# Four-layer graph network on one core: the third layer's projections as three products of rounded halves, a shared arena, and new instruction sequences

## The reference

```python
x = _layernorm(x + _L0_gnn_ref(x, adj, ...))   # attention, 4 heads of 64
x = _layernorm(x + _L1_gnn_ref(x, adj, ...))   # tanh-scored graph layer, 4 heads of 256, gated
x = _layernorm(x + _L2_gnn_ref(x, adj, ...))   # the 32-wide layer: 8 heads of 32
x = _layernorm(x + _L3_gnn_ref(x, adj, ...))   # attention, 4 heads of 64
```

```python
m = embs @ map_w.T + map_b
n = sem / norm                                  # sem: m in heads of 32
cos = jnp.einsum('bhsd,bhtd->bhst', n, n)
cos_adj = (cos > THRESHOLD).astype(embs.dtype)  # THRESHOLD = 0.1
q = (m @ q_w.T + q_b).reshape(b, s, h, dk).transpose(0, 2, 1, 3)
k = (m @ k_w.T + k_b).reshape(b, s, h, dk).transpose(0, 2, 1, 3)
p_attn = jax.nn.softmax(scores, axis=-1) * keep
adj = cos_adj * p_attn
sem_h = (embs @ gcn_map_w.T + gcn_map_b).reshape(b, s, h, hk).transpose(2, 0, 1, 3)
out = jax.nn.relu((adj_h @ sem_h) @ gcn_W.T / (adj_h.sum(-1, keepdims=True) + 1.0))
```

## Time and profile before

| | |
|---|---|
| median of 3 runs | 2848.74 us |
| the profiled execution's own time | 2851.96 us |
| its span, first to last instruction | 2850.2 us |
| TensorE matmul busy | 94% of the span, 21265 instructions |
| VectorE, ScalarE, GpSimd busy | 70%, 48%, 33% |
| mean granted TensorE clock | 0.983 |

### The profile page before, as it was taken

The page is one execution under the profiler, slowest core; times in us unless marked ns, Lnnn a source line. Parts: engine busy times, 40 slices in busy tenths (PEclk is TensorE's granted clock), DMA queues, the critical chain, the costliest instruction groups (busy, mean ns, idle before and its releaser), DMA issues. The chain is left out here.

```text
span 2850.2 us, 61579 instructions
## 1 busy us (share of the span) xinstructions
PE 2669.7 (94%) x21265; PEld 2335.4 (82%) x21265; DVE 1991.9 (70%) x6621; ACT 1381.5 (48%) x3841; POOL 939.0 (33%) x971
## 2 busy tenths in 40 slices
PE   4789999999999999999999999999999999999985
PEld 3778888888888888888888888888888888888873
DVE  3347767777776777777677777767777776777764
ACT  0234545545454554555455445545544554554442
...
DMA packets 44480, 29.76 MB, mean 10 GB/s; under 512 B 21264, under 2 KB 44048, under 8 KB 44432
## 3 DMA queue, kind: packets, MB, share of 16 engines
...
...
## 5 line engine op out<-in xcount | busy, mean ns | idle before, releaser
L176 POOL TENSOR_SCALAR l_ve<-l_mv 128x2 f32<-128x2 f32 x128 | 42.6, 333 | 1048.7 <-DVE l_mv L161 1048.6
L1229 ACT ACTIVATE b<-b,s_sh 128x256 f32<-128x256 f32 x512 | 255.6, 505 | 109.7 <-DVE s_sh L418 109.7
L245 PE MATMUL bank<-a32r 128*128 128x256 f32 x1024 | 304.4, 297 | 3.6 <-issue 2.2
L1480 POOL TENSOR_TENSOR a32r<-a,a32r 128x512 fp32r<-128x512 f32 x128 | 180.9, 1413 | 339.8 <-ACT a32r L1179 337.4
L247 PE MATMUL bank<-a32r 128*128 128x256 f32 x1024 | 289.6, 283 | 0.0
L246 PE MATMUL bank<-a32r 128*128 128x256 f32 x1024 | 289.2, 282 | 0.0
L1485 POOL TENSOR_TENSOR a32r<-a,a32r 128x512 fp32r<-128x512 f32 x128 | 166.4, 1300 | 301.7 <-ACT a32r L1175 301.7
L418 DVE CUSTOM_DVE_ANT_0 b<-bank,s_add 128x256 f32<-128x256 f32 x512 | 185.9, 420 | 84.5 <-issue 59.2
L413 DVE TENSOR_TENSOR a32r<-bank,a32r 128x512 fp32r<-128x512 f32 x128 | 85.6, 689 | 208.2 <-ACT a32r L1216 114.9
L245 PEld LDWEIGHTS bank<-a32r 128*128 128x128 f32 x1024 | 195.2, 191 | 37.3 <-issue 22.9
L1388 DVE SCALAR_TENSOR_TENSOR b<-bank,b 128x256 f32<-128x256 f32 x512 | 188.2, 420 | 33.5 <-PE bank L1083 31.3
(11 more groups left out here) (248 smaller groups left out, 8777.2 us busy)
## 6 DMA issues: line engine op xcount, KB each, us to landing
...
```

Of the source, the lines that this page charges most:

```text
L176: pool.tensor_scalar(N.ve[:, :], N.mv[:, :, 1], LN_EPS, None, ALU.add).then_inc(N.eps.sem, 1)
L245: pe.matmul(out, w[0], x[0], start=first, stop=False)
L1229: last = act.activation(S.e[:, n, it, :], S.e[:, n, it, :], ACT.Exp, bias=S.sh[:, it, h:h + 1], scale=-1.0, accum_out=S.sums[:, it, h:h + 1])
L1480: pool.tensor_tensor(G.wh[h % 2][1], G.whf[:, h % 2, :, :], G.wh[h % 2][0].bitcast(F32), ALU.subtract).then_inc(G.wh_sb.sem, 1)
```

## The change

1. S.xt, S.w_m, S.w_q, S.w_k and S.w_s become pairs of fp32r halves. TensorE's four projections of layer S then go through the three-product branch of pe_product. ScalarE writes S.xt's hi half, and a new VectorE stage b_x_t writes its lo half (dve_lower); b_m, b_q, b_k and b_sem wait for that one. The weights' halves are made in dve_setup.
2. Layer A's probabilities, exponentials, q, k and v move from the tile a32 into the tile "arena", whose places are also seen as fp32r under the name arena_r, and there lie over buffers of layer G. a32 shrinks from 10 to 5 places, and a32r (22 places) becomes arena_r.
3. All four lists of ORDER are replaced. ScalarE's g_wh for heads 2 and 3 gets one more wait, on the product that last read the buffer it writes.

```diff
+ARENA, ARENA_AT = 22, 16512
...
     "PE": [
-        ("g_gate_x", 1), ("a_x_t", 0), ("g_ha_t", 1), ("d_k", 2), ("g_gate", 1), ("d_scores_0", 2), ("d_v", 2),
...
+        ("g_ha_3_1", 1), ("g_ha_3_0", 1), ("d_k", 2), ("g_ha_t", 1), ("a_x_t", 0), ("g_gate_x", 1), ("d_q", 2),
...
+        arena = sb("arena", [P, ARENA * T * NODES])
+        arena_r = nc.alloc_sbuf_tensor_at("arena_r", [P, ARENA * T * NODES], F32R, offset=ARENA_AT)
...
-        a32, a32r = places("a32", 10, F32), places("a32r", 22, F32R)
-        b32 = places("b32", 13, F32)
+        a32, a32r, plain = places("a32", 5, F32), places_of(arena_r), places_of(arena)
+        b32, b32r = places("b32", 13, F32), places("b32r", 2, F32R)
...
-        A.e, A.pt, A.qt, A.kt, A.v, A.xb = a32(0, 4), a32(4, 4), a32(4), a32(5), a32(8), x1
+        A.e, A.pt, A.qt, A.kt, A.v, A.xb = plain(10, 4), plain(16, 4), plain(14), plain(15), plain(8), x1
...
-        S.m, S.sq, S.u, S.xt, S.sem = (b32(n) for n in (4, 5, 6, 7, 0))
+        S.m, S.sq, S.u, S.sem = (b32(n) for n in (4, 5, 6, 0))
+        S.xt = split(b32r, 0)
...
-        S.w_m, S.w_q, S.w_k, S.w_s = (sb(f"s_w_{n}", [P, T, DIM])[:, :, :] for n in "mqks")
+        S.w_m, S.w_q, S.w_k, S.w_s = (split_sb(f"s_w_{n}", [P, T, DIM]) for n in "mqks")
...
             def g_wh(g, h):
                 act.wait_ge(G.wh_f.sem, G.wh_f.at(g, h + 1))
+                if h >= 2:
+                    act.wait_ge(G.p_psum.sem, G.p_psum.at(g, h - 1))
                 act.activation(G.wh[h % 2][0], G.whf[:, h % 2, :, :], ACT.Copy).then_inc(G.wh_hi.sem, 1)
...
-                    act.activation(S.xt, view(BB[2]), ACT.Copy).then_inc(S.x_t_sb.sem, 1)
+                    act.activation(S.xt[0], view(BB[2]), ACT.Copy).then_inc(S.x_t_hi.sem, 1)
...
+                elif stage == "b_x_t":
+                    dve.wait_ge(S.x_t_hi.sem, S.x_t_hi.at(g))
+                    dve_lower(dve, BB[2], S.xt).then_inc(S.x_t_sb.sem, 1)
```

More of the change, by code:

```diff
@@ L45 @@
 BANK = 512
+ARENA, ARENA_AT = 22, 16512
 ORDER = {
     "PE": [
-        ("g_gate_x", 1), ("a_x_t", 0), ("g_ha_t", 1), ("d_k", 2), ("g_gate", 1), ("d_scores_0", 2), ("d_v", 2),
[3 rows of a table removed]
-        ("d_out", 2), ("a_out", 0), ("b_m", 1), ("g_adj_t", 0), ("b_k", 1), ("b_sem", 1), ("g_x_t", 0), ("b_q", 1),
[7 rows of a table removed]
+        ("g_ha_3_1", 1), ("g_ha_3_0", 1), ("d_k", 2), ("g_ha_t", 1), ("a_x_t", 0), ("g_gate_x", 1), ("d_q", 2),
+        ("g_gate", 1), ("d_scores_0", 2), ("d_v", 2), ("a_k", 0), ("d_scores_1", 2), ("a_q", 0), ("a_v", 0),
+        ("a_scores_0", 0), ("d_probs_0", 2), ("d_probs_1", 2), ("d_probs_2", 2), ("d_probs_3", 2), ("a_scores_1", 0),
+        ("d_values_0", 2), ("b_x_t", 1), ("a_probs_0", 0), ("a_probs_1", 0), ("d_values_1", 2), ("a_probs_2", 0),
+        ("a_probs_3", 0), ("a_values_0", 0), ("a_values_1", 0), ("d_out", 2), ("a_out", 0), ("b_m", 1), ("b_sem", 1),
+        ("g_adj_t", 0), ("b_q", 1), ("g_x_t", 0), ("b_k", 1), ("g_z_0", 0), ("b_unit_t", 1), ("g_c", 0),
[6 rows of a table added]
+        ("d_x_t", 1),
@@ L63 @@
     ],
     "ACT": [
[L65 to L69, removed]
[4 rows of a table removed]
+        ("b_copy_6", 2), ("g_wh_3", 1), ("g_p_2", 1), ("g_s_3", 1), ("b_relu_1", 2), ("g_a_3", 1), ("g_p_3", 1),
@@ L74 @@
+        ("d_x_t", 2), ("g_ha", 1), ("d_k", 2), ("g_ha_t", 1), ("a_x_t", 0), ("d_q", 2), ("g_gate", 1),
+        ("d_exps_0", 2), ("a_k", 0), ("d_exps_1", 2), ("d_exps_2", 2), ("a_q", 0), ("d_exps_3", 2), ("d_probs_0", 2),
+        ("d_probs_2", 2), ("a_exps_0", 0), ("a_exps_1", 0), ("a_exps_2", 0), ("a_exps_3", 0), ("a_probs_0", 0),
+        ("b_x_t", 1), ("a_probs_2", 0), ("a_o_copy", 0), ("g_x_t", 0), ("b_k", 1), ("b_q", 1), ("g_z_0", 0),
[4 rows of a table added]
     ],
     "DVE": [
-        ("b_stats", 2), ("g_p_3", 1), ("b_norm_out", 2), ("g_diff", 1), ("g_ha_t", 1), ("a_x_t", 0), ("g_gate", 1),
@@ L77 @@
-        ("d_mask_0", 2), ("g_mix", 1), ("g_sum", 1), ("d_mask_1", 2), ("d_v", 2), ("g_stats", 1), ("d_norm_p_0", 2),
[3 rows of a table removed]
-        ("d_stats", 2), ("a_sum", 0), ("b_m", 1), ("a_stats", 0), ("b_square", 1), ("a_norm_out", 0), ("g_x_t", 0),
-        ("b_unit", 1), ("b_sem", 1), ("g_z_0", 0), ("g_adj_t", 0), ("b_mask_0", 1), ("g_c", 0), ("b_mask_1", 1),
[5 rows of a table removed]
-        ("b_factors", 1), ("g_p_2", 0), ("b_scale", 1), ("b_sum", 1),
+        ("b_factors", 2), ("b_copy_5", 2), ("b_copy_7", 2), ("g_p_2", 1), ("g_a_3", 1), ("b_scale", 2), ("b_sum", 2),
@@ L89 @@
+        ("b_stats", 2), ("b_norm_out", 2), ("g_p_3", 1), ("g_diff", 1), ("a_x_t", 0), ("g_ha_t", 1), ("g_gate", 1),
+        ("d_mask_0", 2), ("g_mix", 1), ("d_v", 2), ("g_sum", 1), ("d_mask_1", 2), ("g_stats", 1), ("d_mask_2", 2),
[3 rows of a table added]
+        ("d_sum", 2), ("a_sum", 0), ("a_stats", 0), ("b_m", 1), ("b_square", 1), ("a_norm_out", 0), ("d_stats", 2),
+        ("g_x_t", 0), ("b_sem", 1), ("b_unit", 1), ("g_z_0", 0), ("g_c", 0), ("b_mask_0", 1), ("b_mask_1", 1),
[5 rows of a table added]
     ],
     "POOL": [
-        ("g_wh_3", 2), ("g_a_3", 2), ("b_rstd", 3), ("b_mask", 2), ("g_x_ha", 2), ("g_adj", 1), ("g_rstd", 2),
@@ L92 @@
-        ("d_bias", 3), ("b_keep", 2), ("a_bias", 1), ("d_mask", 2), ("a_rstd", 1), ("b_inorm", 2), ("d_rstd", 3),
-        ("g_wh_0", 1), ("g_a_0", 1), ("g_a_1", 1), ("a_mask", 0), ("g_wh_1", 1), ("g_a_2", 1), ("g_wh_2", 1),
-        ("b_sums", 2),
+        ("g_wh_2", 2), ("g_a_2", 2), ("b_sums", 3), ("g_wh_3", 2), ("g_a_3", 2), ("b_mask", 2), ("b_rstd", 3),
+        ("b_keep", 2), ("g_x_ha", 2), ("a_mask", 1), ("a_bias", 1), ("d_bias", 3), ("g_adj", 1), ("g_rstd", 2),
+        ("a_rstd", 1), ("b_inorm", 2), ("g_wh_0", 1), ("g_a_0", 1), ("g_wh_1", 1), ("d_rstd", 3), ("d_mask", 2),
@@ L95 @@
+        ("g_a_1", 1),
     ],
@@ L529, in build @@
         C.ident, C.ident_bf = sb("ident", [P, P]), sb("ident_bf", [P, P], BF16)
-        C.ones, C.minus_one, C.minus_half = sb("ones", [P, P]), sb("minus_one", [P, 16]), sb("minus_half", [P, 16])
+        C.minus_one, C.minus_half = sb("minus_one", [P, 16]), sb("minus_half", [P, 16])
         x_in, x_loaded = sb("x_in", [P, T, DIM]), signal("x_loaded", 16)
@@ L544, in places, with places_of @@
         def places(name, count, dt):
-            t = sb(name, [P, count * PLACE], dt)
+            return places_of(sb(name, [P, count * PLACE], dt))
+        def places_of(t):
             def at(first, n=1):
@@ L644, in build @@
         W = Names()
[L646 removed]
+        C.ones = plain(20)[:, 0, 0:P]
+        W.w, W.attn, W.r = a32(0, 4), plain(10, 4), b32(0, 4)
         W.a_w = b32(0, 4).rearrange("p h t n -> p (h t n)").rearrange("p (t n) -> p t n", t=T)
[L648 removed]
+        W.fc, W.g1, W.g2, W.map, W.q, W.k, W.gm = plain(8), plain(9), b32(4), b32(5), b32(6), b32(7), b32(8)
         W.g1_t, W.q_t, W.k_t = W.g1, W.q, W.k
@@ L760, in c_bias @@
                 for kc in range(T):
-                    last = pe.matmul(b[:, 0:HG], C.ones[:, :], W.ab[:, kc, :], start=(kc == 0), stop=(kc == T - 1))
+                    last = pe.matmul(b[:, 0:HG], C.ones, W.ab[:, kc, :], start=(kc == 0), stop=(kc == T - 1))
                 return last
@@ L791, in dve_setup @@
             for jt in range(T):
-                dve.tensor_scalar(W.gb_rows[:, jt, :], C.ones[:, :], W.gb[:, jt:jt + 1], None, ALU.mult)
+                dve.tensor_scalar(W.gb_rows[:, jt, :], C.ones, W.gb[:, jt:jt + 1], None, ALU.mult)
             for h in range(HG):
@@ L1468, in _ @@
             pool.memset(C.minus_half[:, :], -0.5).then_inc(const_ready, 1)
-            pool.memset(C.ones[:, :], 1.0).then_inc(const_ready, 1)
+            pool.memset(C.ones, 1.0).then_inc(const_ready, 1)
             pool.wait_ge(const_ready, 3)
```

5 lines of the change are left out of this document (2 added, 3 removed), and 40 rows, old and new, of the table ORDER.

## The result

The changed kernel takes **2815.09 us**, the median of 4 runs (2814.03 to 2816.07), against 2848.89 for the kernel before on the same chip (2847.84 to 2849.53): a ratio of 0.9882, 95% interval 0.9865 to 0.9899, 34 us less. The forecast was 2804 and faster, with a range of 2755 to 2838. So the sign and the range held and the size was 11 us too good. The attribution behind it was worse than the sum, as the experiments show.

What follows compares the result with a forecast made beforehand. TensorE's sequence with short waits was taken as the bound: -1.32 projections, -0.3 waits, +0.2 edges, -1.42 us a period, -44 over 31; +1 setup, -2 fill and drain gave 2807, less 3.2 to the median 2804 us, range 2755 to 2838.

Steps and rivals of the forecast that it cites:

- What bounds the kernel: Whole body: one long TensorE sequence with short waits, 3.5 us of waits in a period of 83.36 us.
- The term of the projections: Layer S's four projections on TensorE: 1.40 us each instead of 1.73, gaining 1.32 us a period (0.88 to 1.44).
- eaten at g_x_t: Rival: shorter projections cover less of the chain from a_out, g_x_t waits 1.0 us longer; 2835 us, chance 0.17.
- The waits: TensorE's waits under the new lists: 3.2 us a period in sum against 3.5 before, a gain of 0.3.
- d_probs_2: TensorE's wait for VectorE's a_v, g_norm_out (1.05) and d_norm_p_1 (0.86): 0.7 to 0.8 us, before 0.95.
- a_probs_0: TensorE's new wait for VectorE's a_mask_2, a_mask_3 and 0.86 of a_norm_p_0 (2.15 us): 0.6 us.
- b_values_1: TensorE's new wait because b_factors (1.35 us) now precedes VectorE's b_copy_5 and b_copy_7: 0.55 us.
- slower, by GpSimd: Rival: GpSimd's new run of stages ends 2 us later, g_p_1 waits 1.8 us a period; 2861 us, chance 0.05.
- The other work: TensorE: scores of D and A no longer neighbours, one more block of small products, about +0.2 us a period.
- Setup, fill and drain: Outside the full periods: +1 us for setup copies (0 to 2.8), -2 us for fill and drain.
- The last step: From profiled execution to median: 3.2 us taken off 2807, giving 2804 us.
- tests named beforehand: Signs: period 81.9 us, b32r spacing 0.114 to 0.119, no a_scores_1 wait, four named idle times, no GpSimd releaser before g_p_1.

Runs made afterwards that it cites:

- e1: The changed kernel with layer S's four projections in fp32 again, new lists and arena kept: 2826.99 us, ratio 0.9917 to the kernel before.
- e2: The changed kernel with the four lists of the kernel before, plus b_x_t on VectorE: 2844.90 us, ratio 0.9980 to the kernel before.
- e7: The changed kernel with the hi*lo product left out of layer S's four projections: 2815.66 us, ratio 0.9880 to the kernel before.
- e3: The changed kernel with VectorE's d_norm_out moved behind g_c and GpSimd's d_rstd behind b_inorm: 2797.70 us, ratio 0.9819 to the kernel before.

## Why the prediction was right, and where it was wrong

**What bounds the kernel: right.** The body is TensorE's sequence with short waits. The period was forecast to fall by 1.42 us and fell by 1.05 (28 periods, 29.4 us).

**The term of the projections was mis-sized, and its cover mis-read.** I took 4 x (1.73 - 1.40). The rows above give 1.42 and 1.43 for b_m and b_sem. b_q and b_k stand beside transpositions; without their waits (0.32 and 0.20, below) they take 1.52, the upper one of my bounds, against 1.64 and 1.78 before as they stood. Together the four save 1.0, not 1.32. Of this 0.5 arrives (e1), because 0.3 is paid back before g_x_t and 0.2 before g_z_0. These two waits were in the sum, but under another part, so that the text credits the projections with nearly the whole gain. e1 and e2 show 23 us for the lists and 6 to 12 for the projections. The rival "eaten at g_x_t" was right as a mechanism for this term (e2, e7) and wrong for the whole, since the lists' gain lies elsewhere.

**The waits, one by one.** In the table (means of 22 periods) a wait is the distance to the next stage's start less the same distance where nothing is waited for, so the part under the last record is in it.

| wait before | before | predicted | after |
|---|---|---|---|
| a_scores_1 | 0.76 | 0 | 0 |
| b_x_t | 0.41 | 0 | 0 |
| d_x_t, d_q | 0.74 | 0 | 0 |
| a_values_0 | 0.14 | 0 | 0 |
| d_probs_2 | 0.85 | 0.75 | 0.27 |
| d_values_0 | 0 | 0.4 | 0.42 |
| a_probs_0 | 0 | 0.6 | 0.55 |
| g_x_t | 0.53 | 0.3 | 0.32 |
| g_z_0 | 0 | 0.3 | 0.20 |
| b_unit_t | 0 | 0.3 | 0 |
| b_values_1 | 0 | 0.55 | 0 |
| a_scores_0, d_values_1, a_values_1 | 0 | 0 | 0.43 |
| b_transpose_4 | 0 | 0 | 0.50 |
| sum | 3.43 | 3.2 | 2.69 |

What was said to go went. d_values_0, a_probs_0 and g_x_t came out within 0.05, a_probs_0 with luck: two masks of 0.69 and 0.86 are 2.24, not the 2.15 I wrote, and would have given 0.7. d_probs_2 was over-priced by 0.5: of this 0.33 is g_norm_out ahead of it, which took 0.72 and not the 1.05 that I took from a row where it had a GpSimd instruction beside it; the other 0.15 is not traced.

**b_values_1: the step failed.** I moved b_factors with the duration of the earlier trace rows, 1.35 us. After, it takes 0.65, because its last instruction is short:

```profile
1297.90 0.16 DVE L1453 TENSOR_TENSOR s_den<-s_dsum,s_sd 128x16 f32<-128x16 f32 x1
...
1298.38 0.17 DVE L1457 TENSOR_TENSOR s_fac<-s_pw,s_kp 128x16 f32<-128x16 f32 x1
```

The 0.87 us of the earlier trace rows were a wait in disguise: in the kernel before a lower half on GpSimd ran beside it and ended at the same time, at 1404.35:

```profile
1403.03 1.32 POOL L1485 TENSOR_TENSOR a32r<-a,a32r 128x512 fp32r<-128x512 f32 x1
```

**b_transpose_4: missing from the prediction.** For the same reason d_norm_out, which I moved by its steps as they stood, became 0.5 longer. I looked at GpSimd's new list for what TensorE waits for in it, and not for what VectorE would meet beside it. The rival "slower, by GpSimd" looked at the same instructions, but at g_p_1, where nothing of TensorE's waits for them. This wait costs 15 us (0.50 x 31; e3, without it, is 17 us faster).

**The other work: +0.2 predicted, about +0.7 measured.** The period fell by 1.05, while the waits fell by 0.74 and the projections by 1.0; so 0.7 came on. Summed over the steps of 22 periods of each kernel, without the waits, it is 0.22 in the three-product work outside the projections, 0.16 in the scores, 0.19 in the values, 0.10 in layer D's fp32 products and 0.02 in the transpositions. It is at the edges between kinds of TensorE work, since the steps inside a stage are the same in both kernels (0.117 and 0.118 on average in three-product work). In the changed kernel the first two instructions of a_out, behind the fp32 product d_out, start 0.30 apart and the following ones 0.12; behind b_cos_1 the same step is 0.23:

```profile
1340.26 0.47 PE L247 MATMUL bank<-l_wo_hi,arena_r 128*128 128x256 f32 x1
1340.56 0.28 PE L248 MATMUL bank<-l_wo_lo,arena_r 128*128 128x256 f32 x1
1340.68 0.28 PE L249 MATMUL bank<-l_wo_hi,arena_r 128*128 128x256 f32 x1
```

```profile
1374.21 0.38 PE L247 MATMUL bank<-arena_r 128*128 128x256 f32 x1
1374.44 0.28 PE L248 MATMUL bank<-arena_r 128*128 128x256 f32 x1
1374.55 0.28 PE L249 MATMUL bank<-arena_r 128*128 128x256 f32 x1
```

I counted one block of small products more. The lists have 13 separate blocks of scores or of values a period where there were 11, and 20 blocks of three-product work where there were 19. That the edges are the 0.7 is worked out from the distances between starts, not isolated by a run.

**Setup, fill and drain.** +2.8, -8 beyond three periods, and -0.5, against +1, nothing and -2. 2.8 was my upper bound for the setup copies, but in e1, which has none of them, the setup is 0.9 us longer than before too, so about 1.9 is theirs, by one execution of each. The fill's gain was not foreseen and is not settled: its waits are other ones than the body's, and its granted clock differs from kernel to kernel.

**The sum.** Per period the waits came out 0.45 us better than forecast, the projections and edges together 0.82 worse, which is the 0.37 by which the period was off; the fill gave 8 us back. The total was nearer than its parts, and that is luck. The last step, 3.2 us off because the profiled execution before lay that much above its median, did not hold either: after, the profiled execution (2814.03) lies 1.1 below the median. Between the two profiled executions the forecast was 7 us too good, between the medians 11. Of the tests named beforehand, the period (80.5 to 82.8 asked, 82.35 found), the spacing on b32r (0.12), a_scores_1, the idle time before d_values_0 and a_probs_0 and GpSimd at g_p_1 came out as said. The wait before b_values_1 did not come, and the one before d_probs_2 is too short to show as idle time in the body.
